# Attention scores of two tokens by two, in 32-by-32 strips of the array

## The reference, cut to what matters

```python
h, hd = (H, dm // H)                      # 16, 16
Q = (x @ Wq.T).reshape(b, s, h, hd)
K = (x @ Wk.T).reshape(b, s, h, hd)
V = (x @ Wv.T).reshape(b, s, h, hd)
scores = jnp.einsum('bshd,bstd->bsht', Q, K) / math.sqrt(hd)
attn = jax.nn.softmax(scores, axis=-1)
out = jnp.einsum('bsht,bstd->bshd', attn, V).reshape(b, s, dm)
return out @ Wfc.T
```

## Time and profile before

| | before |
|---|---|
| median of 3 runs | 1058.15 us (1058.12 to 1059.05) |
| the profiled execution | 1056.94 us |
| its span in the profile | 1055.1 us |
| TensorE (PE) busy | 966.2 us, 92% of the span |
| weight loads (PEld) | 829.3 us, 79% |
| VectorE (DVE) | 621.1 us, 59% |
| ScalarE (ACT) | 493.6 us, 47% |
| GpSimd (POOL) | 384.3 us, 36% |
| second attention, first to last scores | 555.8 to 785 us |

### The profile page before, as it was taken

The page is one execution under the profiler, slowest core; times in us unless marked ns, Lnnn a source line. Parts: engine busy times, 40 slices in busy tenths (PEclk is TensorE's granted clock), DMA queues, the critical chain, the costliest instruction groups (busy, mean ns, idle before and its releaser), DMA issues. The chain is left out here.

```text
span 1055.1 us, 30102 instructions
## 1 busy us (share of the span) xinstructions
PE 966.2 (92%) x11221; PEld 829.3 (79%) x11222; DVE 621.1 (59%) x1446; ACT 493.6 (47%) x1343; POOL 384.3 (36%) x341
## 2 busy tenths in 40 slices
PE   6999999999999999999988999999767888999996
PEld 3466666988999999999966877777656878899995
DVE  3478877763544444444513788888885777344442
ACT  2656665304445445454346786776552440322221
POOL 0535344421222222321203565555552101455552
PEclk9999999899999999999998999999858999999999
DMA  9874471295222222231055755766421620444441
GB/s 336 252 295 122 123 260 46 93 355 149 87 90 90 83 95 88 76 98 60 8 117 83 131 123 138 149 136 124 87 73 55 250 122 20 151 133 139 133 135 35
DMA packets 133008, 135.58 MB, mean 128 GB/s; under 512 B 73868, under 2 KB 122126, under 8 KB 130724
## 3 DMA queue, kind: packets, MB, share of 16 engines
q1 hardware_dynamic: 121668, 90.80, 30.9%
q0 software_dynamic: 11232, 43.27, 12.9%
HBM read 96.21 MB, written 44.77 MB: 134 GB/s over the span
## 5 line engine op out<-in xcount | busy, mean ns | idle before, releaser
L1132 PE MATMUL psall<-rows 128*128 128x128 f32 x1872 | 221.9, 275 | 2.4 <-DVE rows L1186 2.4
L1132 PEld LDWEIGHTS psall<-rows 128*128 128x128 f32 x1872 | 215.3, 192 | 2.9 <-issue 2.8
L1099 POOL DMA_INDIRECT x<-ffn_rows,tok_i x78 | 82.7, 1060 | 242.1 <-DVE rows L1205 141.1
L1144 PE MATMUL psall<-whi,rows 128*128 x624 | 141.0, 379 | 0.0
L1186 DVE COPY rows<-wlo 128x2048 f32 (+1 forms) x78 | 74.9, 960 | 108.4 <-PE psall L1132 102.3
L1144 PEld LDWEIGHTS psall<-whi,rows 128*128 128x128 f32 x624 | 115.7, 190 | 14.1
L1443 DVE STREAM_TRANSPOSE whi<-whi 32x512 f32<-32x512 f32 x128 | 89.8, 701 | 9.0 <-POOL whi L1406 7.7
L277 PE MATMUL psall<-cst 128*128 128x128 f32 x722 | 91.8, 285 | 0.5 <-PEq L1326 0.5
L1523 ACT ACTIVATE whi<-psall 32x512 f32<-32x512 f32 x128 | 75.2, 587 | 30.4 <-PE psall L1652 25.7
L1245 ACT ACTIVATE rows<-psall,vs 128x128 f32<-128x128 f32 x312 | 84.9, 383 | 9.5 <-PE psall L1132 5.9
L277 PEld LDWEIGHTS psall<-cst 128*128 128x128 f32 x722 | 87.7, 200 | 0.7 <-issue 0.6
(11 more groups left out here) (251 smaller groups left out, 1680.1 us busy)
## 6 DMA issues: line engine op xcount, KB each, us to landing
ffn_rows<-mod_rows SPq DMA_DIRECT2D x2, 4096.0 KB
wlo<-in_W SPq DMA_DIRECT2D x2, 4096.0 KB, 17.3
whi<-in_w SPq DMA_DIRECT2D x5, 1024.0 KB, 8.5
whi<-mod_rows SPq DMA_DIRECT2D x4, 1024.0 KB, 14.3
ffn_rows<-rows SPq DMA_DIRECT2D x8, 512.0 KB
ffn_rows<-x SPq DMA_DIRECT2D x8, 512.0 KB
wlo<-attn_rows SPq DMA_DIRECT2D x32, 128.0 KB, 3.6
v_turn<-wlo SPq DMA_DIRECT2D x32, 128.0 KB, 3.1
```

Source lines behind the costliest of these rows:

```text
L1099: eng.indirect_dma_start(xin[j % DEEP], None, src_d, bass.IndirectOffsetOnAxis(tok_i[:, j:j + 1].bitcast(U32), 0), bounds_check=T, oob_is_ ...
L1132: last = eng.matmul(b_up[t.par][f // 4][:, (f % 4) * P:(f % 4 + 1) * P], w_now[:, c, f * P:(f + 1) * P], inT[t.par][:, c * P:(c + 1) * P], ...
L1144: last = eng.matmul(b_dn[t.par][:, 0:D], hidT[t.par][:, f * P:(f + 1) * P], w_down[:, bass.ds(e, 1), f, :].rearrange("p o n -> p (o n)"), ...
```

## The change

The scores are computed for two tokens by two instead of eight by eight. For each group g and row strip k there are four products, one per quarter q: stationary 16 x 32 (two tokens' queries), moving 16 x 32 (their keys), written to partitions 32q to 32q + 31, bank k, columns 32g to 32g + 31. The scores of a tile then lie as 128 partitions x 4 banks x 128 columns, just what is wanted. One activation copies them, at the head of ScalarE's list in every step.

```diff
-        b_s = psall[:, 0:4 * 512].rearrange("p (g n) -> p g n", g=GR)
+        b_s = psall[:, 0:4 * 512].rearrange("p (k n) -> p k n", k=TB)[:, :, 0:4 * 32]
...
-                def compact(quads, done):
-                    def stage(t):
-                        eng.wait_ge(c_["ss"], t + 1)
-                        wait_some(eng, c_["et"], t - 2)
-                        for q in quads:
-                            rows_q = slice(32 * q, 32 * q + 32)
-                            last = eng.activation(sc[t % 3][rows_q], b_s[rows_q, :, 32 * q:32 * q + 32], ACT.Copy)
-                        if done:
-                            last.then_inc(c_["comp"], 1)
-                    return stage
+                def compact(t):
+                    eng.wait_ge(c_["ss"], t + 1)
+                    wait_some(eng, c_["et"], t - 2)
+                    eng.activation(sc[t % 3].rearrange("p (k g) n -> p k (g n)", k=TB), b_s, ACT.Copy).then_inc(c_["comp"], 1)
...
                     for g in range(4):
                         for k in range(TB):
-                            at, tok = slice(k * QD, k * QD + HD), slice(32 * p + 8 * g, 32 * p + 8 * g + 8)
-                            last = eng.matmul(b_s[:, 4 * k + g, :], zqk[b % 2][at, tok, :].rearrange("p t h -> p (t h)"),
-                                              zk[b % 2][at, tok, :].rearrange("p t h -> p (t h)"), start=True, stop=True)
+                            at = slice(k * QD, k * QD + HD)
+                            for q in range(4):
+                                tok = slice(32 * p + 8 * g + 2 * q, 32 * p + 8 * g + 2 * q + 2)
+                                last = eng.matmul(b_s[32 * q:32 * q + 32, k, 32 * g:32 * g + 32], zqk[b % 2][at, tok, :].rearrange("p t h -> p (t h)"),
+                                                  zk[b % 2][at, tok, :].rearrange("p t h -> p (t h)"), start=True, stop=True)
```

More of the change, by code:

```diff
@@ L1546, in keep_logits @@
                     eng.activation(key3[:, t, :], one_of(b_lg, t), ACT.Copy).then_inc(c_["key"], 1)
-                tile_steps([(LAG_MX, compact((0, 1), False)), (LAG_N, shift_h), (LAG_V, keep_v), (LAG_EX, exps), (LAG_H, keep_h1T),
-                            (LAG_MX, compact((2, 3), True)), (LAG_QK, keep_qk), (LAG_PV, keep_oT), (LAG_H, keep_logits), (LAG_X, rstd2)],
-                           [(LAG_MX, compact((0, 1, 2, 3), True)), (LAG_N, shift_h), (LAG_V, keep_v), (LAG_EX, exps), (LAG_QK, keep_qk),
+                tile_steps([(LAG_MX, compact), (LAG_N, shift_h), (LAG_V, keep_v), (LAG_EX, exps), (LAG_H, keep_h1T),
+                            (LAG_QK, keep_qk), (LAG_PV, keep_oT), (LAG_H, keep_logits), (LAG_X, rstd2)],
+                           [(LAG_MX, compact), (LAG_N, shift_h), (LAG_V, keep_v), (LAG_EX, exps), (LAG_QK, keep_qk),
                             (LAG_X, rstd2), (LAG_H, keep_h1T), (LAG_PV, keep_oT), (LAG_H, keep_logits)])
```

## The result

The changed kernel takes 1120.26 us (median of four runs, 1118.44 to 1124.08) where the kernel before takes 1058.13 us: 1.058 times as long, with a 95% interval of 1.056 to 1.061. That is 62 us slower, where 14 us faster was forecast. It lies 54 us beyond the range. The profiled execution, the slowest of the four, took 1124.08 us, with a span of 1122.3 us.

What follows compares the result with a forecast made beforehand. TensorE's pace plus waits bound the middle, VectorE the plain step and end. Middle -8.6, filling -4.2, end -7.9 and scores 26 x 0.25 sum to -14.2 us: median forecast 1043.9 us, range 1036 to 1066.

Steps and rivals of the forecast that it cites:

- The bound: Second attention: TensorE's pace plus waits in the middle stretch, VectorE in the plain step and from 736.3 us on.
- "issue" row: TensorE's waits in the middle stretch with no cause shown: 0.5 us of 10.0, assumed to go.
- Compaction: ScalarE's four copies per tile, 2.35 us, become one of 0.60 us; ScalarE loses 1.75 us per step, by itself worth nothing.
- Middle, filling and end: Three stretches of the second attention where waits would go: -8.6 us in the middle, -4.2 filling, -7.9 at the end.
- Scores: TensorE's slot of 128 small matmul records per tile: 1.35 us at 8.9 ns each, +0.25 us per tile over 26 tiles.
- The prediction's own sign of being wrong: The scores slot on TensorE at 1.9 us or more, or TensorE's waits moving to norm2 in the same amount.
- The rival on the other side: TensorE's scores slot: spacing grows over 128 records in a row, 3.3 us per further ns; 1073 to 1107 us, chance 0.18.
- the break-even of 13.3 ns: Scores spacing per pair, a slot of 1.91 us, at which 0.80 us per tile cancels the 20.7 us gain.
- the cases of 14.3 ns and of 4.5 ns: Scores spacing on TensorE: 14.3 ns gives a 2.04 us slot, 1061.7 us, chance 0.13; 4.5 ns gives about 1036, chance 0.05.
- The Trainium skill's floor: Matmul starts on TensorE never under about 25 ns apart: scores slot 3.4 us, kernel 1097 us; weighed against line 770's 8.9 ns.
- The clock: TensorE's granted clock, 0.74 in the mean at the end, may fall earlier; part of a rival of 1050.6 us, chance 0.17.

Runs made afterwards that it cites:

- the run with 16 products: The changed kernel with 16 score products per tile again, no instruction added, single copy kept, three quarters of scores wrong: 1039.57 us, 0.981 of before.
- the run with 144 idle products: The kernel before, four copies kept, with 144 idle column-strip products per tile ahead of the scores: 1333.33 us, one run.

## Why the prediction was wrong

**The bound.** Right as far as it went: TensorE's pace, VectorE in the plain step, the late second half of the copies. But a resource was left out. Six blocks in 30.8 us are one per 5.1 us, and in the runs that wanted more they came one per 4.3 to 4.7 us in the mean. So the kernel before already stood at nine tenths or so of what TensorE's program was supplied with. The page of before shows the queue with its 76 blocks, and its trace had two stops inside groups, 0.52 us at 735.40 and 0.72 us at 751.33. The first is the "issue" row, and the prediction let it go "by assumption".

**Compaction.** Right. The single copy takes 0.60 us, and ScalarE lost 55.7 us.

**Middle, filling and end: the gain.** Near in its sum, 20.7 us forecast against 20.5 in the run with 16 products, but partly by luck. By its parts, from the starts of the first scores and of the projections in the profiles of before and of that run, the middle gave 121.62 - 113.71 = 7.9 us (forecast 8.6), the end 90.16 - 82.42 = 7.7 (7.9), and filling only 46.45 - 45.79 = 0.7 (4.2): the waits for the copy went there too, but 3.7 us of stops stand in their place where before had 1.0. And some 2.3 us of the gain are that run's narrower products.

**Scores: the step that failed.** "The slot becomes 128 x 8.9 ns + 0.21 = 1.35 us, or +0.25 us per tile." The slot of an unbroken group is 1.22 us, so the price of the products on the array was right, even high. The term was wrong in kind: the cost of a product was taken to be what it occupies of the array, and each record with its weight load also takes two of the 256 instructions of a block. 96 more records per tile are 192 instructions, three quarters of a block, and per batch 3 blocks. Measured, a batch takes 40.8 us with them and 29.0 without (the run with 16 products), that is 2.9 us per tile where the forecast had 0.25. Over the kernel the sum had 26 x 0.25 = 6.5 us, and the two runs are 1.058 and 0.981 of before, some 81 us apart, with the slower clock behind the stops in it. The prediction's own sign of being wrong, a slot of 1.9 us or more, came true with the stops: at 707.90 it is 712.00 - 707.90 = 4.10 us.

**The rival on the other side** had the place and nearly the name, "the supply of small matmuls", with 0.18. Its mechanism was wrong, though: it let the spacing grow with the length of a run, and spoke against itself from the earlier trace rows, where spacing doesn't grow. It doesn't here either; 64 pairs are half a block, too few to show what happens at the end of one. The array's own spacing, 9.5 ns, stayed under the break-even of 13.3 ns. That also puts aside the cases of 14.3 ns and of 4.5 ns.

**The Trainium skill's floor** ("TensorE: Matmul & The Clock Gate", section "Wait — 56ns, not 53.3ns?"). By the rule weighed in the prediction, 25 ns from start to start, the slot would have been 3.4 us. Unbroken it was 1.22 us, so the rule doesn't hold for 32 x 32 corners in turn, and the time that it would have given, 1097, was nearer by accident.

**The clock** was feared for the end only. It fell in the middle too, in the mean to 0.87 from 625 to 800 us; behind the stop of 2.75 us it was 0.50.

## What to carry to other kernels

Count instructions as well as time: where TensorE's unrolled program runs through 256 instructions in less than some 4.5 us (here blocks came one per 4.3 to 4.7 us in the mean, 3.5 us at the shortest), the next block may not be there, and the stop shows as "issue" inside a group of like instructions. A change that cuts matmuls into smaller ones should be held against that rate first, step by step as well as in the mean, and the two stops inside groups in the trace of before were a warning. When a change pairs a gain with a cost, look whether the order of a list gives a part of the gain for nothing: here one line gave 7 us.

## What the runs showed of the hardware that I had not expected

- TensorE's program comes in blocks of 256 instructions, 128 pairs of weight load and matmul, and one block followed another by 3.46 to 5.14 us where 128 pairs stood between two stops, 4.65 us in the mean of the run with 144 idle products. The Trainium skill ("Runtime: NRT & Kernel Launch", section "Instruction fetch mechanics") states the blocks of 256 instructions and 16 KB, and the trace agrees; it also says that crossing a block costs little and is mostly hidden, and there the runs differ: a stop of 2.08 us at the end of a block on which TensorE worked for 1.93 us.
- Taking some 61,000 packets of 64 B off the DMA engines changed the time by nothing that these runs can tell (1.054 of before, 1.049 to 1.060, against 1.058).
- A product of 16 x 32 by 32 in a 32 x 32 corner costs 9.5 ns per record with its weight load (1.22 us for 128), in float32, start and switch included.
- A stop of 2.75 us was followed by a granted clock of 0.50, and `values` took 1.91 us where it takes 1.03.
